# Routing counts read at a unit's head, places spread before buffers are cleared, spare matrix products retimed, and the last expert's first tile finished alone

## What is computed

```python
h = tok(x)                                   # 32 x 36 patches -> 256 features, plus a class token and positions
h = concat([h, txt], axis=1)                 # 32 x 69 tokens of 256
h = h + attn(layernorm(h))                   # 16 heads of 64
h = h + ffn(layernorm(h))                    # mixture of 8 experts, top 2

# ffn, T = 2208 tokens, cap = 690 slots per expert
top_v, top_i = top_k(xt @ w_g, 2)            # two experts per token
probs = softmax over the two
rank = cumsum(one_hot(top_i), in order of choice, then token) - 1     # the token's place in its expert
keep where rank < cap
exp_batches[e] = tokens in order of place
out = sum over kept (e, place): prob * (gelu(exp_batches[e] @ c_fc[e]) @ c_proj[e])
```

## Time and profile before

| | us |
|---|---|
| median of 3 runs | 712.69 (712.24 to 714.86) |
| the profiled execution | 714.18 |
| its span, first to last instruction | 712.4 |
| PE busy | 684.5 (96%) |
| DVE busy | 505.3 (71%) |
| ACT busy | 295.1 (41%) |
| POOL busy | 276.4 (39%) |
| mean granted clock of TensorE | 0.990 |

### The profile page before, as it was taken

One profiled execution on the slowest core, in us unless ns is written; L12 is line 12 of the kernel. 1 busy time (PEld: TensorE's weight loads), 2 busy tenths in 40 slices (PEclk: granted clock), 3 DMA queues, 4 the chain that ended last, 5 costly groups with the idle time before them and its releaser, 6 DMA issues.

```text
span 712.4 us, 16922 instructions
## 1 busy us (share of the span) xinstructions
PE 684.5 (96%) x6655; PEld 650.1 (91%) x6655; DVE 505.3 (71%) x1159; ACT 295.1 (41%) x652; POOL 276.4 (39%) x294
## 2 busy tenths in 40 slices
PE   7989999999999999999999898999999999999995
PEld 5878899898998989989989898999999999999995
DVE  5978877978879888787877664856666574837461
ACT  4554445535455354553544213433333242515230
POOL 4664010220402204011020443666666666665706
PEclk9999999999999999999999989999999999999998
DMA  8831000000000000000000413354453544444202
GB/s 261 263 89 27 2 1 18 19 15 4 19 18 18 12 8 18 18 14 13 10 19 19 135 34 98 94 97 97 93 133 68 142 89 98 100 88 102 25 7 30
DMA packets 51580, 42.99 MB, mean 60 GB/s; under 512 B 25494, under 2 KB 45140, under 8 KB 51516
## 3 DMA queue, kind: packets, MB, share of 16 engines
q1 hardware_dynamic: 20171, 27.85, 12.8%
q0 software_dynamic: 29168, 11.61, 10.4%
q10 hardware_dynamic: 2176, 2.64, 1.2%
HBM read 32.76 MB, written 10.25 MB: 60 GB/s over the span
## 4 chain that ended last, share of the span: by engine, by line
PE 68%; DVE 20%; issue 4%; SPq 2%; ACT 2%; DMA 2%; POOL 1%; POOLq 0%; DVEq 0%; ACTq 0%
PE pair L1507 11%; PE pair L1509 10%; PE pair L1508 10%; PE lone L1507 8%; PE lone L1509 7%; PE lone L1508 7%; PE ct_ps L1635 3%; DVE vals L1123 3%; DVE zsum L1113 3%; DVE top L1104 3%; PE pair L1625 3%; DVE expo L1107 3%; PE vt_ps L1612 2%; SPq L436 2%; PE pair L1678 1%
## 5 line engine op out<-in xcount | busy, mean ns | idle before, releaser
L778 POOL DMA_INDIRECT out<-yrow,held x48 | 100.9, 2102 | 63.2 <-DVE yrow L1468 49.0
L999 ACT ACTIVATE act_f<-pair 128x348 f32<-128x348 f32 (+1 forms) x120 | 49.0, 457 | 92.0 <-PE pair L1509 88.9
L1507 PE MATMUL pair<-xe_hi,fc_hi 128*128 128x348 f32 (+1 forms) x256 | 82.8, 324 | 1.6 <-DVE xe_lo L1438 1.2
L761 POOL DMA_INDIRECT held<-token_rows,found_ix x48 | 69.6, 1449 | 34.5 <-issue 21.5
L1509 PE MATMUL pair<-xe_hi,fc_lo 128*128 128x348 f32 (+1 forms) x256 | 82.7, 323 | 0.0
L1508 PE MATMUL pair<-xe_lo,fc_hi 128*128 128x348 f32 (+1 forms) x256 | 82.7, 323 | 0.0
L1507 PE MATMUL lone<-pj_hi,act_hi 128*116 128x256 f32 (+1 forms) x256 | 72.2, 282 | 0.0
L1509 PE MATMUL lone<-pj_hi,act_lo 128*116 128x256 f32 (+1 forms) x256 | 71.9, 281 | 0.0
L1508 PE MATMUL lone<-pj_lo,act_hi 128*116 128x256 f32 (+1 forms) x256 | 71.8, 280 | 0.0
L842 ACT ACTIVATE expo<-expo 69x552 f32<-69x552 f32 x64 | 42.5, 663 | 55.6 <-DVE expo L1107 54.9
L828 ACT ACTIVATE qkv<-pair,bq_sb 128x276 f32<-128x276 f32 x97 | 47.2, 486 | 33.6 <-PE pair L1509 33.2
(11 more groups left out here) (253 smaller groups left out, 1972.8 us busy)
## 6 DMA issues: line engine op xcount, KB each, us to landing
raw_fc<-c_fc SPq DMA_DIRECT2D x8, 1024.0 KB
raw_pj<-c_proj SPq DMA_DIRECT2D x8, 1024.0 KB
raw<-w_qkv SPq DMA_DIRECT2D x6, 512.0 KB, 10.0
out<-h SPq DMA_DIRECT2D x8, 276.0 KB
token_rows<-sent POOLq DMA_DIRECT2D x7, 285.7 KB, 7.0
raw<-patches SPq DMA_DIRECT2D x3, 384.0 KB, 6.1
raw<-patches ACTq DMA_DIRECT2D x3, 384.0 KB, 6.6
raw<-w_l ACTq DMA_DIRECT2D x1, 1024.0 KB, 6.2
```

Of the source, the lines that this page charges most:

```text
L761: pool.indirect_dma_start(xg[p][0:n, t, :], None, x2_dram, bass.IndirectOffsetOnAxis(ap=found_ix[p][0:n, t:t + 1].bitcast(U32), axis=0), b ...
L778: pool.indirect_dma_start(out, bass.IndirectOffsetOnAxis(ap=xg[p][0:n, t, D:D + 1].bitcast(U32), axis=0), yrow[p][0:n, t, :], None, bounds ...
L999: gelu = act.activation(act_f[f % 2][:, a:b], pair[f % 2][:, h, 0:b - a], ACT.Gelu)
L1507: pe.matmul(dst, l_hi, r_hi, start=(first and n == 0), stop=False)
```

## The change

Six edits. DVE's two reads of the rank bank become a step of their own, `take_counts`; in groups 2 to 7 it stands at the head of unit 0, ahead of the sum of the exponentials. POOL's spread of group 6 moves ahead of the clearing of the gather buffers. The spare products after the logits, after the count and after the last table go from 20, 24 and 80 to 18, 30 and 84. PE gets 8 more spare products between the first turns of gathered rows and the first `expand`; they read `fc_hi`. POOL raises `s_begun` behind the first gather, and DVE waits for it ahead of the first expert's four `low_fc`. In the last expert tile 0 is finished before tile 1 is begun.

```diff
@@ gpsimd
             for g in range(GROUPS):
                 stage_b(g)
+            spread(Step(GROUPS), -2)
             pool.wait_ge(s_h2, GROUPS - 3)
             for i in range(2):
                 pool.memset(xg[i][:, :, :], 0.0).then_inc(s_zeros, 1)
             pool.wait_ge(s_zeros, 3)
             pool.memset(xg[0][:, :, D:D + 1].bitcast(I32), FAR).then_inc(s_blank, 1)
-            spread(Step(GROUPS), -2)
             root_mid(Step(GROUPS), -1)
...
@@ gpsimd, fetch, in the loop over the tiles t
                                             bounds_check=TOKENS - 1, oob_is_err=False).then_inc(s_xg[p][t * 2 // XT], 16)
+                    if t == 0 and st.k is None and st.i + shift == 0:
+                        pool.sem_inc(s_begun, 1)
...
@@ vector
-            def put_place(st, shift):
+            def take_counts(st, shift):
                 bank, nth = use("rank", st, shift, 0)
...
                 wait(dve, s_full[bank], st, nth)
                 dve.tensor_tensor(rank[:, :, :], shared[bank][0:TR, 0:TPG * CHOICES].rearrange("p (t c) -> p t c", c=CHOICES),
                                   carry[0:TR, :].unsqueeze(1).broadcast_to([TR, TPG, CHOICES]), ALU.add).then_inc(s_rank, 1)
...
                 dve.tensor_tensor(carry[:, :], carry[:, :], shared[bank][0:XR, TPG * CHOICES:(TPG + 1) * CHOICES], ALU.add)\
                     .then_inc(s_free[bank], 1)
 
+            def put_place(st, shift):
...
+                wait(dve, s_rank, st, lambda i: i + shift + 1)
                 dve.tensor_tensor(rank[:, :, :], rank[:, :, :], chosen[:, :, :, :].rearrange("p t k e -> p t (k e)"), ALU.mult)\
...
@@ vector, unit(m)
+                if u == 0 and g >= 2:
+                    take_counts(st, -2)
                 if u == 4 and g >= 2:
                     add_table(st, -2)
...
                 if u == 7 and before and not more:
+                    take_counts(st, -1)
                     put_place(st, -1)
...
@@ vector, after the units
             share_last()
+            take_counts(last, -1)
             put_place(last, -1)
...
+            dve.wait_ge(s_begun, 1)
             for q in range(4):
                 low_fc(Step(0), 0, q)
@@ tensor
             logit(last, -1, "proj", yT, wg_mid)
-            spare(20)
+            spare(18)
             count(last, -1)
-            spare(24)
+            spare(30)
             tabulate(last, -1)
-            spare(80)
+            spare(84)
...
             turn_first(0)
+            pe.wait_ge(s_fc_hi, 4)
+            for _ in range(8):
+                pe.matmul(pair[0][:, 0, 0:D], fc_hi[:, 0, 0:128], fc_hi[:, 0, 0:D], start=True, stop=True)
             pe.wait_ge(s_xe_lo, KD)
...
@@ tensor, stage_d
+                together = 1 if st.i == NEXP - 1 and st.k is None else 2
                 for f in range(KF):
                     wait(pe, s_act_lo, st, lambda i: KF * i + f + 1)
-                    for t in range(2):
+                    for t in range(together):
                         done = multiply(st, t, range(f, f + 1))
                         if f == KF - 1:
                             done.then_inc(s_y, 1)
+                for t in range(together, 2):
+                    multiply(st, t, range(KF)).then_inc(s_y, 1)
```

More of the change, by code:

```diff
@@ L384, in program @@
             sem(n) for n in ("s_vt", "s_score", "s_top", "s_sub", "s_exp", "s_zs", "s_zi", "s_val", "s_ctx", "s_c_hi", "s_c_lo"))
+        s_begun = sem("s_begun")
         s_h2, s_h2_out, s_m_ln, s_x2 = (sem(n) for n in ("s_h2", "s_h2_out", "s_m_ln", "s_x2"))
@@ L1241, in pick @@
                                       .broadcast_to([TR, TPG, CHOICES]), ALU.mult).then_inc(s_chosen, 1)
-            def put_place(st, shift):
+            def take_counts(st, shift):
                 bank, nth = use("rank", st, shift, 0)
-                every_choice = [TR, TPG * TOPK, XT + 1]
-                def before(n):
-                    wait(dve, s_place, st, lambda i: PLACED * (i + shift) + n)
                 wait(dve, s_full[bank], st, nth)
@@ L1256, in put_place, with before @@
                     .then_inc(s_free[bank], 1)
+            def put_place(st, shift):
+                every_choice = [TR, TPG * TOPK, XT + 1]
+                def before(n):
+                    wait(dve, s_place, st, lambda i: PLACED * (i + shift) + n)
+                wait(dve, s_rank, st, lambda i: i + shift + 1)
                 dve.tensor_tensor(rank[:, :, :], rank[:, :, :], chosen[:, :, :, :].rearrange("p t k e -> p t (k e)"), ALU.mult)\
```

## The result

The changed kernel takes 702.35 us, the median of four executions (701.67 to 702.5), beside 712.97 us for the kernel before on the same chip (712.24 to 714.86): ratio 0.985, 95% interval 0.9828 to 0.9873. Forecast were 702.7 us, 701.0 to 706.6. The profiled execution took 702.5 us with a span of 700.7 (before 714.18 and 712.4). Run again in two of the three later groups, as again and again2, it took 701.97 and 701.51 us in the median; the kernel before took 712.93, 713.15 and 713.29 in the three.

A forecast was written before the change was run, and what follows sets the result against it. PE, busy 96% of the span, was taken as the bound, so only its waits or slow-clock stretches could give time back. Terms 4.8 + 3.4 + 1.5 + 0 + 0.3 = 10.0 us off 712.69 gave 702.7, range 701.0 to 706.6.

The forecast's parts named there:

- The counts: Unit head, groups 2 to 7: earlier reads remove PE's six waits for DVE's carry, 4.8 us gained.
- rivals 4 and 5: Rival 4: another PE wait replaces the bank's, 707.5, chance 0.07; rival 5: DVE waits for the count, 714.7, 0.02.
- The spread and the clock behind it: Between the parts: group 6's table ready without PE's 2.1 us wait, clock stays up, 3.4 us gained in all.
- the 0.9 that the prediction named: Store of group 7's last rows, only 2.5 us earlier: up to 0.9 of the 3.4 us may be lost.
- Rival 2: Routing of group 7: the clock falls all the same; 705.1, with rival 1 706.6; chance 0.11.
- The eight products: Ahead of the first expand: they fill 1.0 us of a 1.23 us wait; first 24 products gain 1.5 us.
- Rival 1: First expert: the clock does not hold, so 1.5 us is not gained; 704.2, chance 0.12.
- The wait for the first gather: low_fc moves from beside gather 1 to beside gathers 2 and 3: zero, bounds 0.3 gained and 1.3 lost.
- Rival 3: low_fc holds up gathers 2 and 3, two times 0.64 us: 704.0, or 705.3 if all four operations cost; chance 0.07.
- The last expert: Tile 0 ready after 24 products instead of 48, scatters start earlier: 0.3 us gained, between 0 and 1.28.

The follow-up runs named there:

- late_counts: Changed kernel with DVE's two reads of the rank bank back behind unit 0's softmax work in groups 2 to 7: 708.9 us.
- only_spread: Kernel before with one edit alone, POOL's spread of group 6 ahead of the clearing of the gather buffers: 709.27 us.
- plain_spares: Changed kernel with the spare products of before (20, 24 and 80, none ahead of the first expand): 703.39 us.
- best2: Changed kernel with each store of group 7's rows split in two (80 and 12 rows) and without DVE's wait for s_begun: 701.08 us.
- begun2: Changed kernel with POOL raising s_begun behind its third gather instead of its first: 701.63 us.
- no_fill: Changed kernel without the 8 spare products ahead of the first expand: 703.09 us.
- no_begun: Changed kernel without DVE's wait for the first gather (s_begun): 701.83 us.
- late_spread: Changed kernel with POOL's spread of group 6 back behind the clearing of the gather buffers: 704.98 us.
- split: Changed kernel with each of the two stores of group 7's rows issued as two, 80 and 12 rows: 701.41 us.

## Why the prediction was right

**The counts: right in place, too small.** 4.8 us were taken from the waits' rows, 6.3 came (6 x 1.04 of period, 6.6 in late_counts). The mis-sized term is the wait itself, which the row counts from the modelled end. DVE had nothing else late, as forecast; no wait took its place, so rivals 4 and 5 are out. The period of a group is shorter by 1.04 us, where the prediction named 0.8 as its sign.

**The spread and the clock behind it: right.** 3.4 us were forecast between the parts; only_spread has 3.32 from the count to the first `expand`. The 2.1 and the clock's share stood as worked out: choices to count 0.26, DVE's read of the count 1.35 behind the choices where 1.3 was forecast. `found_ix` came 3.8 us earlier behind the count, not 3.4, and the store took 0.5 back, inside the 0.9 that the prediction named and then left out of its sum. Rival 2 did not come in the three profiles of the changed kernel: 1.00 from 392 to 442 us, with the waits of 0.99 and 0.78 on which it stood.

**The eight products: right in size, and not a gain in every execution.** 24 products took 3.92 us instead of 5.40, the 1.5 forecast. The reason given, that they cover the wait, is confirmed only together with the retimed spare products: without the eight alone the profile kept its clock. The prediction took one profiled execution for the rule. A third of the executions of before did not have the clock's 2.8 us (1.5 here and 3.4 - 2.1 = 1.3 between the parts) to give back: 713.4 - 710.6 = 2.8 is what the clusters differ by. That two thirds had it is the chance of the draw, which the prediction did not price. Rival 1 describes plain_spares, not the changed kernel.

**The wait for the first gather: zero forecast, 0.3 lost.** The first gather takes 1.80 us instead of 1.46, and without the wait the first `expand` stands 0.2 to 0.3 nearer the count. The step that failed is the reading of the semaphore: it was taken to rise behind the gather, so that `low_fc` would move beside gathers 2 and 3; it rises ahead of it, and `low_fc` starts with gather 1. Rival 3's mechanism exists at a quarter of its price of 1.3, on one gather alone. Measured, a gather is lengthened once, by about what is left of DVE's operation when it starts. Two gathers of the third expert in the changed kernel, at 0.43 and 0.05 us before the end of an `act_hi`:

```profile
471.67 0.51 DVE L1486 CAST act_hi<-act_f 128x690 fp32r<-128x690 f32 x1
471.75 1.61 POOL L762 DMA_INDIRECT held<-token_rows,found_ix  x1 [0.30 <-issue]
...
473.20 0.52 DVE L1486 CAST act_hi<-act_f 128x690 fp32r<-128x690 f32 x1
473.67 1.31 POOL L762 DMA_INDIRECT held<-token_rows,found_ix  x1 [0.30 <-issue]
```

In the fourteen profiles together, of the second to fifth gathers of an expert that start inside one of DVE's splits (`act_hi`, `act_lo`, `fc_lo`, `pj_lo`), all 91 with less than 0.1 us of it left took 1.31 to 1.32 us, and all 114 with 0.4 to 0.5 left 1.58 to 1.65. The changed kernel's first gather starts 0.22 us into the first `low_fc`, 0.47 left, and takes 0.34 more; before, and in best2, it starts within 0.01 us of an operation's start and takes 1.46, as begun2's first does with no operation running at its start. So the row of 1.46, by which the prediction took zero, was a gather that met `low_fc` at a harmless moment. DVE's wait starts `low_fc` just ahead of the gather, where most of an operation is still to come.

The rule of the Trainium skill that the prediction quotes, SBUF — State Buffer, section "SBUF: two separate sides", has whole instructions take turns at the ports, for two SBUF inputs only against a GpSimd operation that reads SBUF; the prediction left that condition out, and no run shows whether a gather meets it. The lengths agree with the rule in this, that a gather waits out an operation that began first. That a gather in turn holds up DVE for its whole length they do not show: in the changed kernel `low_fc`'s four operations start 0.60 to 0.61 us apart beside a gather of 1.80.

**The last expert: 0.3 forecast, 0.6 to 0.8 found.** The last scatter starts 0.87 us behind its tile instead of 1.28, the 0.4 of the mechanism named. As much again lies behind its start (6.05 to 5.58 us), where the prediction had looked for nothing: without the edit it is 5.98 to 6.09.

**The sum.** 6.3 + 3.3 + 1.5 - 0.3 + 0.8 = 11.6 against the kernel before with its clock fallen (11.6 measured), and 8.8 without the clock's 2.8 (8.8 measured). The forecast's terms, 10.0 together, were 1.6 too small for an execution like the profiled one, at 714.18, from which they were read; and that execution stood 1.5 above the median of 712.69 against which they were set off. The two errors cancel, and that the forecast came within 0.4 us of the time is luck to that extent; the mechanisms do not rest on it.

## What to carry to other kernels

Where an engine reads a result only to free its bank, put the read into the earliest gap of that engine's order, not beside the work that uses the value. Price a wait of a full matrix pipe by the distance of the starts around it, not by its row. Look at the clock of many executions before a fall is counted as a gain, and where a wait goes, look at once which transfer is then the last to land.

## What the runs showed of the hardware

- Whether the clock falls from 1.00 to 0.50 differs between executions of one program: the changed kernel had 0.50 at 42 to 44 us in one of its three profiles and 1.00 in the other two. Of 39 executions of before, 26 had a mean clock of 0.986 to 0.993 and 13 of 0.997. Waits of 0.85 and 1.23 us ahead of the first expert were followed by 0.50 (before), waits of 1.53 and 1.23 (no_fill) were not. What decides it stayed open.
- DVE, waiting for a semaphore that POOL's queue raises behind its first indirect gather, started 0.2 us ahead of that gather's row, and with the semaphore behind the third gather 2.8 us ahead of that one's. Such a semaphore does not tell that the work was done or begun.
- A gather that starts while DVE splits weights or activations takes longer by about what is left of that one operation, less some 0.1 us: 1.31 to 1.32 us with under 0.1 us left (91 gathers in fourteen profiles), 1.58 to 1.65 with 0.4 to 0.5 left (114). Beside `low_fc` the first gather took 1.80 and 1.52 us with 0.47 and 0.19 us left (after, no_begun), and 1.46 where an operation started only 0.01 us ahead of it (before, best2). That DVE's operation is the cause follows from the lengths alone; no run moved DVE's work away from the later gathers.
- From the end of the list to the start of the first gather there are 1.12 to 1.13 us when nothing else is late (before, late_spread, split, best2). What they consist of was not tried.
